# Products that nobody reads, put into the item banks of a two-layer attention kernel

## The reference, cut to what matters

```python
# layer 0: quantised attention to itself, quantised attention to a context of 77 tokens, gated feed-forward
x = attn_q(ln(x), ln(x)) @ wo + bo + x        # 16 heads of 16, q, k, v and probabilities rounded to 8 bits
x = attn_q(ln(x), context) @ wo2 + bo2 + x
a, g = split(ln(x) @ w1 + b1);  x = (a * gelu(g)) @ w2 + b2 + x
# layer 1: rotary attention to the context with a mask, 16 query heads on 4 key heads, then SiLU feed-forward
q, k, v = rms(x) @ Wq, rms(ctx) @ Wk, rms(ctx) @ Wv
x = softmax(rope(q) @ rope(k).T / 8 + mask) @ v @ Wo + x
x = silu(rms(x) @ Wgate) * (rms(x) @ Wup) @ Wdown + x
```

## Time and profile before

| | |
|---|---|
| median of 3 runs | 2564.54 us (2559.13 to 2568.57) |
| the profiled execution: device time | 2568.71 us |
| the profiled execution: span of the instructions | 2566.9 us |
| busy share PE, DVE, ACT, POOL | 78%, 70%, 44%, 36% |
| granted TensorE clock, mean over the span | 0.874 of 2.4 GHz |

### The profile page before, as it was taken

The page is one execution under the profiler, slowest core; times in us unless marked ns, Lnnn a source line. Parts: engine busy times, 40 slices in busy tenths (PEclk is TensorE's granted clock), DMA queues, the critical chain, the costliest instruction groups (busy, mean ns, idle before and its releaser), DMA issues.

```text
span 2566.9 us, 35318 instructions
## 1 busy us (share of the span) xinstructions
PE 2000.9 (78%) x10552; PEld 1439.1 (56%) x10552; DVE 1802.5 (70%) x3327; ACT 1135.9 (44%) x1906; POOL 936.3 (36%) x1629
## 2 busy tenths in 40 slices
PE   3665587878787887879887787979887887878786
PEld 3323265656565565656655565656555565556665
DVE  1566778686777777696778768687878777685632
ACT  1244535545454545535453445445453545444211
POOL 1213334343434434343434424343434434343212
PEclk8666698989998898989989898989888898989888
DMA  7486453635445363535436363544535353625010
GB/s 231 102 162 134 82 121 68 131 62 105 93 81 122 70 134 62 118 76 100 98 71 132 69 135 61 118 78 88 105 77 120 74 120 66 128 55 106 1 36 4
DMA packets 761645, 243.62 MB, mean 95 GB/s; under 512 B 675643, under 2 KB 757295, under 8 KB 761199
## 3 DMA queue, kind: packets, MB, share of 16 engines
q1 hardware_dynamic: 758127, 241.34, 46.3%
q10 hardware_dynamic: 3328, 0.01, 0.1%
HBM read 83.57 MB, written 19.25 MB: 40 GB/s over the span
## 4 chain that ended last, share of the span: by engine, by line
PE 47%; DVE 21%; issue 9%; ACT 8%; SPq 5%; DMA 4%; POOL 4%; DVEq 0%; POOLq 0%; ACTq 0%
PE work L1394 21%; PE work L1404 16%; ACT E L899 4%; DVE scaled_row L1055 4%; DVE Pn L1062 3%; PE rowps L1465 3%; DMA PT<-Pn 3%; PE outps L1450 3%; POOL scs L797 2%; SPq L542 1%; DVE st L1078 1%; DVE hids L1202 1%; DVE scs L1144 1%; ACT hTs L875 1%; DVE scs L1216 1%
## 5 line engine op out<-in xcount | busy, mean ns | idle before, releaser
L1055 DVE TENSOR_SCALAR_CACHE_REDUCE scaled_row<-rowps,der 128x1024 uint8<-128x1024 f32 x512 | 654.0, 1277 | 386.8 <-PE rowps L1465 386.5
L899 ACT ACTIVATE E<-rowps,ebias,der 128x1024 f32<-128x1024 f32 x512 | 614.6, 1202 | 392.5 <-DVE scaled_row L1055 312.1
L731 POOL TENSOR_TENSOR rowden<-rowsum,raw 128x1 f32<-128x1 f32 x512 | 113.3, 221 | 943.6 <-ACT E L899 942.3
L1062 DVE TENSOR_SCALAR Pn<-E,rowinv 128x1024 int16<-128x1024 f32 x512 | 389.8, 761 | 89.0 <-DMA PT<-Pn 65.9
L1465 PE MATMUL rowps<-KC,QP 16*128 16x512 bf16 x1024 | 220.8, 428 | 209.5 <-ACT E L899 197.7
L734 POOL TENSOR_TENSOR rowinv<-rowden,minus 128x1 f32<-128x1 f32 x512 | 333.6, 651 | 92.4 <-POOL rowden L731 92.4
L1394 PE MATMUL work<-hTs,ff_w_sb 128*128 128x256 f32 x1024 | 259.9, 409 | 14.2 <-ACT hTs L875 14.2
L1465 PEld LDWEIGHTS rowps<-KC,QP 16*128 16x128 bf16 x1024 | 49.2, 92 | 375.5 <-ACT E L899 244.4
L1394 PEld LDWEIGHTS work<-hTs,ff_w_sb 128*128 128x128 f32 x1024 | 202.3, 204 | 60.0 <-issue 28.4
L1559 PE MATMUL work<-K,hids 128*128 128x154 f32 x1024 | 153.2, 301 | 31.6 <-DVE scs L1216 19.4
L1559 PEld LDWEIGHTS work<-K,hids 128*128 128x128 f32 x1024 | 136.9, 190 | 50.1 <-DVE scs L1216 26.3
(11 more groups left out here) (143 smaller groups left out, 3267.3 us busy)
## 6 DMA issues: line engine op xcount, KB each, us to landing
VW<-vw_dram SPq DMA_DIRECT2D x32, 640.0 KB, 4.9
KC<-k_dram SPq DMA_DIRECT2D x128, 64.0 KB, 2.4
VB<-v_dram SPq DMA_DIRECT2D x64, 128.0 KB, 3.1
PT<-Pn SPq DMA_TRANSPOSE x512, 3.1
V<-v_dram SPq DMA_DIRECT2D x16, 320.0 KB, 3.7
vw_dram<-scs SPq DMA_DIRECT2D x32, 154.0 KB
K<-k_dram SPq DMA_DIRECT2D x16, 308.0 KB, 3.2
K<-k_dram SPq DMA_DIRECT2D x32, 154.0 KB, 3.4
```

Of the source, the lines that this page charges most:

```text
L731: nc.gpsimd.tensor_tensor(rowden[:, n:n + 1], rowsum[:, n:n + 1], raw[:, DW1:DW1 + 1], ALU.mult).then_inc(row_den.sem, 1)
L899: nc.scalar.activation(E[:, slot, :], rowps[n % 2][:], ACT.Exp, bias=ebias[:, n:n + 1], scale=der[:, AL1:AL1 + 1], accum_out=rowsum[:, n:n ...
L1055: nc.vector.tensor_scalar(scaled_row[:, n % 2, :], rowps[n % 2][:], der[:, NAL1:NAL1 + 1], 3.0e38, ALU.mult, ALU.min, accum_out=ebias[:, n ...
L1062: nc.vector.tensor_scalar(Pn[:, n % 2, :], E[:, ring(n)[0], :], rowinv[:, n:n + 1], 255.0, ALU.mult, ALU.min).then_inc(row_round.sem, 1)
```

## The change

The diff is long, for it also replaces the way in which the order is written down: `places`, `AT` and `Beside` go, and a string for each engine (`TURNS`) says which part takes the next turn. Compared instruction by instruction, ACT, POOL and SP have the same instructions in the same order with the same waits. DVE has the same instructions in the same order; the four reciprocals per step of layer 1's sums wait on a semaphore of their own, `h_sums`, where they waited on `h_link`. TensorE has the same instructions in the same order, and between them new ones: `bank_free` now puts products into the bank that it has just waited for.

```diff
+WARM = {
+    ("high", 2): 1, ("high", 10): 1, ("high", 14): 2, ("high", 22): 2, ("low", 0): 1, ("low", 1): 1, ("low",
+    2): 1, ("low", 5): 1, ("low", 9): 2, ("low", 10): 2}
...
+TURNS = {
+    "PE": (
+        "rvhrhhrhprpprppvhrhhrhhrllhrhhvhrhhhhrllrhhhrllvhhrhhhhhrllhhrhhllrvllrhrhrhhllrlllvhrlhhrllhrhrvlrl"
+        "lrllrhrvlrllrlr"),
...
-        HIGH_LINKS = 6
+        HIGH_LINKS = 2
+        h_sums = count("h_sums", 4)
...
                     act_done[c].wait(pe, unit[c], 0)
                     if c in dve_done:
                         dve_done[c].wait(pe, unit[c], 0)
+            for _ in range(WARM.get((chain, i), 0)):
+                nc.tensor.matmul(work[bank][:, 0:CH], wq[:, 0, 0:P], wq[:, 1, :], start=True, stop=True)
             return work[bank]
...
+        def high_sums(dve, u, runs):
+
+            for n in range(4):
+                yield
+                h_exp.wait(dve, u, n + 1)
+                nc.vector.tensor_reduce(lsum[:, 1, n, :], sc1[:, n], AX.X, ALU.add).then_inc(h_sums.sem, 1)
+                h_sums.wait(dve, u, n + 1)
+                nc.vector.reciprocal(rsum[:, 1, n, :], lsum[:, 1, n, :]).then_inc(recip_ready.sem, 1)
```

More of the change, by code:

```diff
@@ L51 @@
 HIGH_ITEMS = (
-    [("ffo", "D", 7.6, 0, None), ("tr2", "A", 0.6, 4.5, "ffo")] + [("wq", "D", 1.9, 1.2, "tr2")] * 4
-    + [("sc0", "D", 1.3, 1.2, "wq")] * 4 + [("sc1", "D", 1.3, 0, "sc0")] * 4
[3 rows of a table removed]
-    + [("gate", "A", 1.9, 1.2, "tr3")] * 4 + [("up", "D", 1.9, 0.5, "gate")] * 4 + [("down", "D", 7.6, 1, "up")])
-BEHIND = {("high", "down"): ("low", "g", 0.1)}
+    [("ffo", "D", 4), ("tr2", "A", 1)] + [("wq", "D", 1)] * 4 + [("sc0", "D", 1)] * 4 + [("sc1", "D", 1)] * 4
+    + [("pt0", "A", 1), ("pt0", "D", 1), ("pt0", "A", 1), ("pv0", "D", 4)]
@@ L60 @@
+    + [("pt1", "A", 1), ("pt1", "D", 1), ("pt1", "A", 1), ("pv1", "D", 4), ("tr3", "A", 1)]
+    + [("gate", "A", 1)] * 4 + [("up", "D", 1)] * 4 + [("down", "D", 1)])
 ITEMS = {"pre": PRE_ITEMS, "low": LOW_ITEMS, "high": HIGH_ITEMS}
-STARTS = {"pre": 2.0, "low": 2.0 * LAG + 3.5, "high": 0.5}
 BANKS = 3
-US_PER_HALF = 1.85
-PAIR_GAP = 2.0
+WARM = {
+    ("high", 2): 1, ("high", 10): 1, ("high", 14): 2, ("high", 22): 2, ("low", 0): 1, ("low", 1): 1, ("low",
+    2): 1, ("low", 5): 1, ("low", 9): 2, ("low", 10): 2}
@@ L67, in item @@
+PRE_AT = {"tr": (4.0, 4.9), "q": (5.5, 6.9), "k": (6.3, 7.8), "v": (7.2, 8.7)}
 def item(items, name, n=0):
     return [i for i, x in enumerate(items) if x[0] == name][n]
[L72 to L87, removed]
[L88 to L111 removed]
@@ L114, with item_order @@
-AT, ORDER = places(2 * ROWT - 1.5)
+def item_order():
+    begins = {c: {sum(x[2] for x in ITEMS[c][:i]): i for i in range(len(ITEMS[c]))} for c in ITEMS}
+    turn, out = {c: 0 for c in ITEMS}, []
+    for letter in TURNS["PE"]:
+        c = PARTS_OF.get(letter)
+        if c:
+            if turn[c] in begins[c]:
+                out.append((c, begins[c][turn[c]]))
+            turn[c] += 1
+    return out
+ORDER = item_order()
 def banks(chains):
@@ L129, in emptied, with take_turns, by_time @@
     return sum(x[1] == engine for x in ITEMS[chain][:i + 1])
-class Beside:
-    def __init__(self, *parts):
-        self.parts = [[float("-inf"), part] for part in parts]
[L139 to L144, removed]
-            part[0] = next(part[1], None)
-            if part[0] is None:
-                self.parts.remove(part)
-    def rest(self):
-        self.until(float("inf"))
+def take_turns(order, parts):
+    for part in parts.values():
+        next(part)
+    for letter in order:
+        if letter in parts:
+            next(parts[letter], None)
+    assert all(next(part, "end") == "end" for part in parts.values())
+def by_time(*parts):
+    parts = [[next(part), part] for part in parts]
+    while parts:
+        part = min(parts, key=lambda x: x[0])
+        part[0] = next(part[1], None)
+        if part[0] is None:
+            parts.remove(part)
 class Count:
@@ L545, in attn_sync @@
             for n in range(ROWT):
-                beside.until(2 * n)
+                yield 2 * n + 0.01
                 if tiles(parts, n - 2):
@@ L1584, in high_pe @@
                     silu_ready.wait(pe, u, 4)
[L1585 removed]
+                    yield from project_rows(ps, hid1, Wdown, FC, h_filled.sem, whole=True)
         @block.tensor
```

367 lines of the change are left out of this document (157 added, 210 removed), and 3 rows, old and new, of the table HIGH_ITEMS.

## The result

The changed kernel took 2541.51 us (median of 8 runs, 2536.40 to 2545.77), the kernel before 2554.06 us (8 runs, 2546.73 to 2568.57). The ratio is 0.9943 with a 95% interval of 0.9918 to 0.9968: 0.6% faster, 12.6 us between the medians and 14.6 us by the ratio. The forecast was "no change", 2563 us, and it was wrong, though 2541.5 lies just inside its range of 2540 to 2582 us. Part of the distance to the predicted time is the baseline: the three runs of before that the prediction had are among the eight and have their median at 2564.5; the five that came later lie at 2546.7 to 2555.4, with a median of 2552.3.

A forecast was written before the change was run, and what follows sets the result against it. No engine bounds it alone; TensorE bounds `pt0` to `pv1` and `gate` to `down`. Terms: -3 us (`tr0` to `pv1`, 14 steps) + 2 us (step 1) = -1 us; against 2564.5, forecast 2563 us, range 2540 to 2582.

The forecast's parts named there:

- The step that failed: `tr0` to `pv1`, steps with full clock through `q2`: 25.2 us in three of five, 26.6 us in two.
- The floor: `tr0` to `pv1`: the best step before, 25.21 us, was taken as the time without a second fall.
- The price of a product: Any place on TensorE: one added product takes 0.46 us at the full clock, 0.94 us at the low clock.
- the eleven that have cover: 11 of the 14 products per step lie in waits or beside DVE and cost nothing; uncovered, 5.1 us a step.
- The slow half at 26.1: `tr0` to `pv1`, half the steps: low-clock `q2`, pair open for 0.9 us, no second fall, 26.1 us.
- The share of steps that keep the clock through `q2`: a half: At `q2`: half of the steps keep the full clock through it, taken as the middle between none and all.
- `sc2[2]`, +0.1 us: At `sc2[2]`: its one product makes it 0.46 us late, mostly absorbed by a later wait; 0.1 us a step.
- `gate` unchanged: Before `gate`: it starts at the low clock as before, first eight records 3.75 us; gain 0 us.
- The gain put at 28 us there for a clock kept up: Rival before `gate`: clock stays up there too, some 2 us a step, -28 us, 2524 us; chance 0.08.
- the clock stays up from `tr0` to `pv1`: Rival: all 14 steps at 25.2 us, -14 and +2, 2552 us; chance 0.17, shared with fewer low stretches.
- The slow one: Rival ahead of `pt0`: the pair lies open at 1.2 GHz, 27.4 us a step, 2585 us; chance 0.15.
- Other luck: Rival between `gate` and `down`: shifts change second low stretches, +10 to -17 us; fewer shares chance 0.17, worse 0.03.

The follow-up runs named there:

- e2_q2_pt0: Changed kernel with only the four products ahead of `tr0`, `q2` and `pt0`; ratio to the kernel before 0.9929.
- e6_low12: Changed kernel with only one product ahead of `tr0` and one ahead of `q2`, none ahead of `pt0`; ratio to the kernel before 1.0005.
- e3_tail: Changed kernel with only the six products ahead of `sc2[6]`, `sc2[7]` and `tr3`; ratio to the kernel before 0.9998.
- e4_rest: Changed kernel with only the four products ahead of `wq[0]`, `wo`, `sc1[0]` and `sc2[2]`; ratio to the kernel before 1.0008.
- e1_none: Changed kernel with an empty table, so none of the 224 products, new order and `h_sums` kept; ratio to the kernel before 1.0013.
- e7_pt0: Changed kernel with only the two products ahead of `pt0`; ratio to the kernel before 0.9929.
- e16_gate_only: Changed kernel without its products, with three new ones behind `tr3`'s transposes, ahead of `gate`; ratio to the kernel before 0.9878.
- e9_turns: Changed kernel without its products, with six transposes ahead of `pt0`; ratio to the kernel before 0.9861.
- e10_one: Changed kernel with only one product, ahead of `pt0`; ratio to the kernel before 0.9884.
- e13_wait: Changed kernel without its products; `pt0` also waits until POOL has cast the query of `q2`; ratio to the kernel before 1.0110.
- e17_gate_turns: Changed kernel without its products, with eleven unread transposes behind `tr3`'s transposes, ahead of `gate`; ratio to the kernel before 0.9991.

## Why the prediction was wrong, point by point

- *The step that failed* is "three in five of these take 25.2 us, two in five fall again before `pv0` and take 26.6": the floor of 17.2 us from `pt0` to `pv1`, and the second falls behind a fast `q2`. The changed kernel takes 16.58 to 16.64 us there in all 14 steps, and not one falls. What stands ahead of `pt0` was forecast rightly: 7.99 us after `tr0` with a fast `q2` and near 8.9 with a slow one; measured 7.36 and 8.2 to 8.3, which is 7.9 and 8.8 with the mark moved by 0.56 us.
- *The falls.* The forecast took them over from the steps of before, though it had written of the slow half that with the pair it does "not fall a second time". Behind a fast `q2` the pair fills the 1.67 us of waiting for POOL's `pps` down to 0.57 us, and that is the place from which the clock fell (e2_q2_pt0 against e6_low12, and the count of 52 and 17 steps above).
- *The floor.* The 25.21 us of the best step hold 0.45 us in which `sc2[1]` waits for DVE's `pTs`, which the sum did not see. With a fast `q2` the score row behind it comes earlier, and DVE has its `pTs` long before (`pt0` begins at 685.25 and 535.45 us):

```profile
688.09 0.68 DVE L1234 COPY pTs<-work 128x512 f32<-128x512 f32 x1
```

```profile
536.65 0.69 DVE L1193 COPY pTs<-work 128x512 f32<-128x512 f32 x1
```

It ends 3.5 us after the start of `pt0` in the best step before and 1.9 us after it now, while `sc2[1]` wants it some 3 us after. In the four steps with a slow `q2` it is the time of the pair that lets DVE get there. In both the wait is gone, worth 0.6 us a step. Together: the measured 24.23 us are 24.79 with the mark put back where it was, and the forecast was 26.03, so 1.24 us a step or 17 us were missed. As an estimate from these numbers, some 8 us are the floor, 6 the falls, 3 the larger share of fast `q2`, and 1 the `sc2[2]` that cost nothing (18 in all, so right to a microsecond).
- *The price of a product and the eleven that have cover.* Right. e3_tail (six products) and e4_rest (four) stay within 0.3% of nothing. `wq` to `tr0` did grow past the 24 us named as a warning (24.15 us at the least, where 23.6), but by the product that stands ahead of `tr0` itself: e4_rest, with `wo` and `sc1[0]` and without that one, has 25.02 us in the mean where e1_none has 25.08.
- *The slow half at 26.1.* Right for the kernel with the pair alone: behind a slow `q2` e7_pt0 has 26.03 us from `tr0` to `pv1`, as a mean of 25.2 to 25.4 and of 26.2 to 26.6. In the changed kernel these four steps took 24.8, where 26.1 less the 0.6 of the mark would be 25.5.
- *The share of steps that keep the clock through `q2`: a half.* Ten of 14. By itself it earns nothing: e6_low12 has 11 of 14 and the time of before.
- *`sc2[2]`, +0.1 us, and step 1, +2.* Too small to be told apart; e4_rest shows no loss.
- *`gate` unchanged.* Right in its size: `tr3` to `gate` 5.05 us (5.21), the first eight records 3.64 us (3.73). The gain put at 28 us there for a clock kept up was of the right kind: e16_gate_only measures 0.9878, some 31 us.
- *Rivals.* The one that came is "the clock stays up from `tr0` to `pv1`", priced at 2552, which is 12 us less than before; the measured difference is 12.6 to 14.6. It held fully in ten steps, and in four the low stretch is over before `pt0`. The slow one, the pair at 1.2 GHz and open, does occur in e7_pt0 (`pt0` 9.6 to 10.0 us after `tr0`, in nine steps), and with what it saves behind `pt0` such a step takes 26.2 to 26.6 us and not 27.4. "Other luck" is no small term: seven steps of the changed kernel have a second low stretch between `gate` and `down` where nine had one, and in e7_pt0, e9_turns and e10_one, with four, none and none, it carries more of the gain than the stretch from `tr0` to `pv1`.
- *That 0.5% is what a measurement of this kernel can tell from no change.* Too coarse. The interval came out at a quarter of a per cent to either side, so 0.6% was told from nothing.

Taken together: low clock costs by where it lies. Behind `pt0`, where TensorE bounds, it costs up to 3 us a step. Ahead of `pt0` it costs 0.8 us a step in the changed kernel (24.8 against 24.0) and more where the pair itself runs in it (26.2 to 26.6 in nine steps of e7_pt0). In the change under test the products round `q2` keep the clock up to the score row in ten steps, and the pair keeps it from falling right after; `tr0` to `pv1` is near 24.2 us with both, 26.4 and 26.0 with either alone. That all of it comes from the products and not from the rewriting is shown by e1_none, that the pair is needed behind a fast `q2` by e6_low12, that standing still in its place makes things worse by e13_wait. Why the pair alone, one product or six transposes reach the same time or a better one with fewer low stretches behind `gate` is open.

## What to carry to other kernels

A product that nobody reads pays where it fills a pause just ahead of work that TensorE bounds; ask not whether the clock falls but in which stretch its low time lands, and measure each filler alone, for of the 14 here ten did nothing. Then read the whole step and not only the place of the filler: two kernels with the same ratio had their gain in different stretches. Fill a pause with as many as end before the next real instruction, counted at the low clock: three products gained where five spent the gain on a held-up score row. Keeping the clock up at one place can move the fall to a dearer one, so a change that makes one instruction fast is no gain until the whole step is shorter.

## What the runs showed of the hardware

TensorE standing still for 1.66 us or more ahead of ten transposes, behind a `q2` at the full clock, was followed by 6.8 us at 1.2 GHz in 17 of 17 steps; with two products in that place and 0.57 to 0.86 us of standing still in 0 of 52. Steps that differ by a few tenths of a microsecond up to `pv1` differ in whether a second low stretch follows between `gate` and `down` (e7_pt0 against e9_turns); that the tenths decide it was not shown. Transposes did not bring the clock back in a 4 us pause (e17_gate_turns: 3.64 us in the mean for the eight records behind them, 2.73 in e16_gate_only with three products). With six of them between the score row and `pt0` no step fell behind `pt0` (e9_turns, all 14 at PEclk 0.99 or 1.00), though eight of the 14 would hardly have fallen without them. Why the same kind of work counts in one place and not in the other was not settled.
